# First gates loaded on their own, down weights split earlier, a half's w2 products a step later, beta added in PSUM

## What is computed

```python
# layer 0: per batch, expert weights fside (8 of them) and a shared gate sg
g = einsum('bsd,edf->ebsf', h, Wg);  u = einsum('bsd,edf->ebsf', h, Wu)
expert_outs = einsum('ebsf,efd->ebsd', silu(g) * u, Wd)
x = x + (1 - sg) * einsum('be,ebsd->bsd', gating_probs, expert_outs) \
      + sg * ((silu(h @ Sg) * (h @ Su)) @ Sd)
# layer 1: per batch, by language id
a = relu(x @ W1[lang] + b1[lang]) @ W2[lang] + b2[lang]
z = x + a
x = x + (z - mean(z)) * rsqrt(var(z) + 1e-5) * gamma[lang] + beta[lang]
```

## Time and profile before

| | us |
|---|---|
| median of 3 runs | 300.93 (300.68 to 301.18) |
| the profiled execution | 301.38 |
| its span, first to last instruction | 299.6 |
| PE busy | 291.7 |
| DVE busy | 265.6 |
| ACT busy | 228.6 |
| POOL busy | 18.1 |

### The profile page before, as it was taken

The page is one execution under the profiler, slowest core; times in us unless marked ns, Lnnn a source line. Parts: engine busy times, 40 slices in busy tenths (PEclk is TensorE's granted clock), DMA queues, the critical chain, the costliest instruction groups (busy, mean ns, idle before and its releaser), DMA issues.

```text
span 299.6 us, 5010 instructions
## 1 busy us (share of the span) xinstructions
PE 291.7 (97%) x1518; PEld 145.1 (48%) x1518; DVE 265.6 (89%) x587; ACT 228.6 (76%) x511; POOL 18.1 (6%) x31
## 2 busy tenths in 40 slices
PE   8899999999999999999999999999999999999993
PEld 2344444444444444444444444444444444588782
DVE  4999999998989898988978999989998898977795
ACT  6788888787878787877787788877878775676770
POOL 2200010300000000000001010001100011000001
PEclk9999999999999999999999999999999999999998
DMA  7963031441000000000011001010001100000001
GB/s 204 394 288 109 0 112 24 104 119 47 2 2 0 0 2 0 0 2 1 1 22 20 15 0 38 11 25 16 4 0 40 26 17 9 3 35 3 0 2 35
DMA packets 16620, 12.99 MB, mean 43 GB/s; under 512 B 10818, under 2 KB 14674, under 8 KB 16594
## 3 DMA queue, kind: packets, MB, share of 16 engines
q1 hardware_dynamic: 16162, 12.40, 13.6%
q10 hardware_dynamic: 432, 0.27, 0.3%
HBM read 10.83 MB, written 1.05 MB: 40 GB/s over the span
## 4 chain that ended last, share of the span: by engine, by line
PE 96%; DVE 2%; ACT 1%; issue 0%; POOL 0%; POOLq 0%; DVEq 0%; ACTq 0%
PE gate_ps L374 11%; PE moe_ps L420 10%; PE moe_ps L423 10%; PE moe_ps L421 10%; PE gate_ps L377 10%; PE gate_ps L382 10%; PE up_ps L405 10%; PE up_ps L400 10%; PE up_ps L397 10%; PE moe_ps L455 1%; PE adapt_ps L449 1%; DVE hidden L625 1%; DVE w_lo L611 1%; PE adapt_ps L432 0%; ACT h_hi L529 0%
## 5 line engine op out<-in xcount | busy, mean ns | idle before, releaser
L524 ACT ACTIVATE silu<-gate_ps 128x512 f32<-128x512 f32 (+1 forms) x160 | 88.6, 554 | 58.3 <-PE gate_ps L382 57.4
L625 DVE SCALAR_TENSOR_TENSOR hidden<-silu,up_ps 128x512 f32<-128x512 f32 (+1 forms) x160 | 100.7, 629 | 26.2 <-PE up_ps L405 16.8
L631 DVE TENSOR_TENSOR h_lo<-hidden,h_hi 128x512 f16<-128x512 f32 (+1 forms) x160 | 102.8, 643 | 0.2
L529 ACT ACTIVATE h_hi<-hidden 128x512 f16<-128x512 f32 (+1 forms) x160 | 92.8, 580 | 2.5 <-DVE hidden L625 1.8
L420 PE MATMUL moe_ps<-h_hi,w_hi 128*128 128x512 f16 (+1 forms) x160 | 57.2, 358 | 1.2 <-DVE w_lo L611 1.2
L374 PE MATMUL gate_ps<-x_hi,w_hi 128*128 128x512 f16 (+1 forms) x160 | 57.8, 361 | 0.0
L377 PE MATMUL gate_ps<-x_lo,w_hi 128*128 128x512 f16 (+1 forms) x160 | 57.7, 361 | 0.0
L382 PE MATMUL gate_ps<-x_hi,w_lo 128*128 128x512 f16 (+1 forms) x160 | 57.7, 360 | 0.0
L405 PE MATMUL up_ps<-gx_hi,w_lo 128*128 128x512 f16 (+1 forms) x160 | 57.2, 358 | 0.1
L397 PE MATMUL up_ps<-gx_hi,w_hi 128*128 128x512 f16 (+1 forms) x160 | 57.2, 358 | 0.0
L400 PE MATMUL up_ps<-gx_lo,w_hi 128*128 128x512 f16 (+1 forms) x160 | 57.2, 358 | 0.0
(11 more groups left out here) (74 smaller groups left out, 144.1 us busy)
## 6 DMA issues: line engine op xcount, KB each, us to landing
w_full<-weights SPq DMA_DIRECT2D x8, 768.0 KB, 8.4
affine_sb<-affine SPq DMA_DIRECT2D x16, 128.0 KB, 2.9
x_full<-xT SPq DMA_DIRECT2D x3, 256.0 KB, 8.2
x<-x_blocks SPq DMA_DIRECT2D x48, 16.0 KB, 1.8
out_dram<-result SPq DMA_DIRECT2D x3, 256.0 KB, 2.1
w_full<-weights SPq DMA_DIRECT2D x4, 128.0 KB, 3.4
w2b_sb<-w2b SPq DMA_DIRECT2D x16, 16.5 KB
w_full<-weights SPq DMA_DIRECT2D x1, 256.0 KB, 4.6
```

The costliest lines, as they stand in the source:

```text
L524: nc.scalar.activation(silu_slot(n), gate_ps[n % 2][:, 0:STEPS[n][4]], ACT.Silu, scale=1.0 / W_SCALE).then_inc(silu_ready, 1)
L529: nc.scalar.activation(h_slot(h_hi, n), hidden_slot(n), ACT.Copy).then_inc(h_hi_ready, 1)
L625: nc.vector.scalar_tensor_tensor(out=hidden_slot(n), in0=silu_slot(n), scalar=HIDDEN_RESCALE, in1=up_ps[n % 2][:, 0:STEPS[n][4]], op0=ALU. ...
L631: nc.vector.tensor_tensor(h_slot(h_lo, n), hidden_slot(n), h_slot(h_hi, n), ALU.subtract).then_inc(h_lo_ready, 1)
```

## The change

- The gates are laid out with the shared gate first and then expert by expert. ACT's queue loads the first 32 columns (shared gate and expert 0) first of all, under a semaphore of their own, and then x's second half of tile 0. SP loads x's first half as its second transfer, and the rest of the gates behind weight piece 1. POOL waits for the rest of the gates only before the `coef` of the other experts.
- Weight piece 4 (down weights of expert 0) is split in step 1 on ACT and DVE. Group 1's gated x is made in step 2: on ACT two quarters before `h_hi` of step 1 and two behind it, on DVE all four before `h_lo` of step 1.
- For tile 1 POOL waits for the third `w_lo` only before `x_lo`, not before `x_hi`.
- `back_at` of the last job is 6 instead of 5, and with it `stats_at` and what follows.
- In the tail the transposes of x2 stand behind the w2 products. To each bank a product of a row of ones (row 32 of `adapt_h`) with the beta row is added, and the result reads x2 plus beta from PSUM. DVE's two additions fall away.

```diff
 def back_at(j):
-    return 4 if j < MOVED else 5
+    return 4 if j < MOVED else 6
...
             load_first(0)
-            sp.dma_start(cols(x_full, 1, HALF), xT[0, :, HALF:]).then_inc(x0_loaded[1], 16)
+            sp.dma_start(cols(x_full, 0, HALF), xT[0, :, 0:HALF]).then_inc(x0_loaded[0], 16)
             for i in (1, 2, 3):
                 load_first(i)
+                if i == 1:
+                    sp.dma_start(gates_in[:, 2 * B:], gates[:, 2 * B:]).then_inc(gates_loaded, 16)
...
             for i, q in tail:
-                nc.tensor.transpose(tail_x2_ps[i][:, 0:D], cols(x2T, q, S), ident[:, :]).then_inc(x2_transposed, 1)
-            for i, q in tail:
                 nc.tensor.matmul(tail_y_ps[i][:, 0:D], cols(x2T, q, S), ident[:, :], start=True, stop=False,
                                  is_transpose=True)
...
+            for i, q in tail:
+                nc.tensor.matmul(tail_x2_ps[i][:, 0:D], cols(x2T, q, S), ident[:, :], start=True, stop=False,
+                                 is_transpose=True)
+            for i, q in tail:
+                nc.tensor.matmul(tail_x2_ps[i][:, 0:D], adapt_h[A:A + 1, 0:S],
+                                 cols(affine_sb[A:A + 1], 2 * (last_tile * BATCHES + q) + 1, D, 1),
+                                 start=False, stop=True).then_inc(x2_transposed, 1)
...
-            act.dma_start(cols(x_full, 0, HALF), xT[0, :, 0:HALF]).then_inc(x0_loaded[0], 16)
+            act.dma_start(gates_in[:, 0:2 * B], gates[:, 0:2 * B]).then_inc(first_gates_loaded, 16)
             nc.scalar.preload_act_table(ACT.Silu)
-            act.dma_start(gates_in[:, :], gates).then_inc(gates_loaded, 16)
+            act.dma_start(cols(x_full, 1, HALF), xT[0, :, HALF:]).then_inc(x0_loaded[1], 16)
...
                 silu_of(n)
-                if n == 0:
-                    first_weight_hi(3)
+                if n < 2:
+                    first_weight_hi(3 + n)
                 if n == 2:
-                    first_weight_hi(4)
+                    gated_x_hi(1, 0)
+                    gated_x_hi(1, 1)
                 if n > 0:
                     hidden_hi(n - 1)
-                if n == 1:
-                    gated_x_hi(1, 0)
-                    gated_x_hi(1, 1)
...
-                if n == 0:
-                    first_weight_lo(3)
+                if n < 2:
+                    first_weight_lo(3 + n)
                 if n == 2:
-                    first_weight_lo(4)
+                    for q in range(BATCHES):
+                        gated_x_lo(1, q)
...
-            for i in range(count):
-                tail_x2_beta(i)
...
-                dve.wait_ge(x2_beta_ready, j + i + 1)
-                norm_result(j + i + 1, t, first + i, BEFORE[j] + i + 1)
+                dve.wait_ge(x2_transposed, i + 2)
+                norm_result(j + i + 1, t, first + i, BEFORE[j] + i + 1, tail_x2_ps[i][:, 0:D])
...
-            pool.wait_ge(gates_loaded, 16)
+            pool.wait_ge(first_gates_loaded, 16)
...
                 pool.wait_ge(x_loaded[t - 1], 16)
-                pool.wait_ge(w_lo_ready, X_AFTER[t])
+                if t > 1:
+                    pool.wait_ge(w_lo_ready, X_AFTER[t])
                 nc.gpsimd.tensor_copy(cols(x_hi, t, N), cols(x_full, t, N)).then_inc(x_rest_hi_ready, 1)
                 pool.wait_ge(x_rest_hi_ready, t)
+                if t == 1:
+                    pool.wait_ge(w_lo_ready, X_AFTER[t])
```

More of the change, by code:

```diff
@@ L201, in build @@
         tail_y_ps = [gate_ps[0], up_ps[0]]
+        first_gates_loaded = sem("first_gates_loaded")
         gates_loaded = sem("gates_loaded")
@@ L672, in norm_scaled, with norm_result @@
                                                op0=ALU.subtract, op1=ALU.mult).then_inc(scaled_ready, 1)
-            def norm_result(rstd_done, t, q, done):
+            def norm_result(rstd_done, t, q, done, x2_beta_q):
                 dve.wait_ge(rstd_ready, rstd_done)
@@ L677, in norm_result @@
                 nc.vector.scalar_tensor_tensor(out=cols(result, t * BATCHES + q, D), in0=cols(scaled, q, D),
-                                               scalar=rstd[:, q:q + 1], in1=cols(x2_beta, q, D),
+                                               scalar=rstd[:, q:q + 1], in1=x2_beta_q,
                                                op0=ALU.mult, op1=ALU.add).then_inc(result_ready, 1)
@@ L693, in job_part @@
                         dve.wait_ge(x2_beta_ready, j + 1)
-                        norm_result(j + 1, t, first + i, BEFORE[j] + i + 1)
+                        norm_result(j + 1, t, first + i, BEFORE[j] + i + 1, cols(x2_beta, first + i, D))
                     if since == out_at + i and (j, i) != LATE_OUT:
@@ L747, in _ @@
                                                op1=ALU.add).then_inc(x2T_ready, 1)
-            norm_result(j, late_t, late_q, BEFORE[-1])
+            norm_result(j, late_t, late_q, BEFORE[-1], cols(x2_beta, late_q, D))
             q = first + 1
@@ L777, in _ @@
             pool.wait_ge(ones_ready, 2)
-            pool.wait_ge(gates_loaded, 16)
-            per_expert = gates_in[:, 0:B * (NE - 1)].rearrange("p (b e) -> p e b", b=B)
-            shared_in = gates_in[:, B * (NE - 1):]
+            pool.wait_ge(first_gates_loaded, 16)
+            shared_in = gates_in[:, 0:B]
             nc.gpsimd.tensor_scalar(rest[:, :], shared_in, -X_SCALE, X_SCALE, ALU.mult, ALU.add).then_inc(rest_ready, 1)
             pool.wait_ge(rest_ready, 1)
-            nc.gpsimd.tensor_tensor(coef[:, 0:B], per_expert[:, 0], rest[:, :], ALU.mult).then_inc(first_coef_ready, 1)
+            nc.gpsimd.tensor_tensor(coef[:, 0:B], gates_in[:, B:2 * B], rest[:, :], ALU.mult).then_inc(first_coef_ready, 1)
             nc.gpsimd.tensor_scalar(coef[:, (NE - 1) * B:], shared_in, X_SCALE, None, ALU.mult)
-            nc.gpsimd.tensor_tensor(coef[:, B:(NE - 1) * B].rearrange("p (e b) -> p e b", b=B), per_expert[:, 1:],
+            pool.wait_ge(gates_loaded, 16)
+            nc.gpsimd.tensor_tensor(coef[:, B:(NE - 1) * B].rearrange("p (e b) -> p e b", b=B),
+                                    gates_in[:, 2 * B:].rearrange("p (e b) -> p e b", b=B),
                                     rest[:, :].rearrange("p (o b) -> p o b", o=1).to_broadcast([P, NE - 2, B]),
@@ L845 @@
     wd = wd.reshape(NE, CHUNKS, P, D).transpose(0, 2, 1, 3).reshape(NE, P, F)
-    gates = np.concatenate([a["fside_Bx8_0"].reshape(1, -1), a["condB_sharedgateprob"].reshape(1, B)], axis=1)
+    gates = np.concatenate([a["condB_sharedgateprob"].reshape(1, B), a["fside_Bx8_0"].T.reshape(1, -1)], axis=1)
     arrays = {
```

## The result

The changed kernel takes 299.02 us (median of 6, 298.30 to 299.82), the kernel before 300.81 (median of 6 in the same place): ratio 0.9938, 95% interval 0.992 to 0.9956, 1.79 us less. Run a second time beside other kernels it took 299.41 us, ratio 0.9956 (0.994 to 0.9972). The forecast was 299.54, with 298.7 to 300.3 around it. Three runs far above their like, one of before at 516.83 us beside e1 to e4, one of before at 1091.87 beside e5 to e8 and one of e12 at 311.72, are left out of the ratios.

A forecast was written before the change was run, and what follows sets the result against it. PE is full in the body, so only its idle time at the start, last tile's second half and tail can give: 0.70 + 0.55 + 0.14 = 1.39 us off 300.93, so 299.54 us, range 298.7 to 300.3.

The forecast's parts named there:

- Part 1: Start: splitting down weights ahead of group 1's gated x removes 1.68 us of stall, 0.68 returns, gain 1.00 us.
- the new wait: Start: PE's product L400 of up(4) waits for DVE's fourth gx_lo, giving back 0.68 us.
- Part 2: Start: reordered gates and x loads make later loads land later, taking 0.3 us off the start's 1.00 us gain.
- s: Start: how much later the loads behind the extra gates issue land, 0 to 0.46 us, taken as 0.3.
- the hold: Start: POOL's x_lo of tile 1 holds DVE's 256-wide w_lo, 1.07 us where two take 0.75 us.
- The late first products: Start: first gate products begin 0.1 to 0.3 us later because x's first half is issued later; swallowed right behind hidden(0).
- Part 3: Last tile's second half: w2 products a step later gain 0.55 us (0.3 to 0.75), with 0.17 us waiting at the up product.
- Part 4: Tail: beta in PSUM and later x2 transposes start L492 0.14 us sooner (0 to 0.22); PSUM source costs nothing.
- A: Start: no new wait at L400, or w_lo beats POOL; start gives 1.0 to 1.68 us, time 298.7; chance 0.15.
- B: Start gives only 0.3 us, with later loads, late first product and h_hi(0) slipping; time 300.2 us; chance 0.15.
- C: Start: TensorE's 2.4 GHz level comes later because of the gap before the gate products, eating the gain; 300.9 us; chance 0.05.
- D: Start: ACT stands behind the down weights' load, free up to about 9.2, then one for one; 302.5 us; chance 0.03.

The follow-up runs named there:

- e1: Only the new order of the splits (down weights in step 1, group 1's gated x in step 2) on the kernel before: 299.67 us, ratio 0.9971.
- e4: Only the tail change (x2 transposes behind the w2 products, beta added in PSUM) on the kernel before: 300.47 us, ratio 0.9994.
- e5: New split order, later w2 products and tail change on the kernel before, with loads, gates and POOL's order as before: 299.48 us, ratio 0.9944.
- e8: The changed kernel with a plain fill in place of POOL's x_lo of tile 1: 298.66 us, ratio 0.9922.
- e12: The changed kernel with the down weights issued behind expert 1's 768 KB load: 301.88 us, ratio 1.0037.
- e2: Only the gates and x loads and POOL's order of the changed kernel, on the kernel before: 300.70 us, ratio 0.9993.
- e3: Only the w2 products of the last job one step later, on the kernel before: 300.20 us, ratio 0.9981.
- e7: The kernel before with a plain fill in place of POOL's x_lo of tile 1: 300.25 us, ratio 0.998.
- e6: The changed kernel measured again, unaltered, beside other kernels: 299.41 us, ratio 0.9956 to the kernel before.
- e9: The changed kernel with the rest of the gates loaded behind the down weights and POOL's other coef behind tile 1's x_lo: 299.01 us, ratio 0.9943.

## Why the prediction was right, and where it was off

**Part 1** was right in mechanism and in size within the interval: 1.00 us forecast before the loads' cost, 1.05 measured alone (0.6 to 1.2 by the ratio), 1.12 between the profiles of before and e5. The list of DVE's operations by their own spacing found both the stall that goes and the one that comes back. The size of the new wait was misstated (0.68 us; 0.40 by its own figures, 0.42 measured in e1 and e5), which leaves the gain of 1.00 as it is.

**Part 2** was forecast at minus 0.30 and measured at plus 0.02. The step that failed is s, the later landing of tile 1's x. I took it as fixed, 0.3 us. In the two profiles of the changed kernel POOL's split of that tile starts at 6.95 and at 8.21 us with the same issues, a scatter four times as large as the term; with e2 (7.01) and e8 (7.81) the four start at 7.50 on average. The six with the old loads start between 7.46 and 7.68, 7.57 on average: POOL is no later. The load itself landed 0.2 us later on average (6.9 to 8.2, 7.1 to 7.5 with the old loads), but a term that the forecast put at nothing makes up for it. The forecast read POOL's wait off one profile, where the load ended it; in those of e3, e4, e5 and e7 the load took 4.0 to 4.2 us (landing at 7.1 to 7.3) and POOL stood on for the third `w_lo`, so that the removed wait gives 0.1 to 0.5 us there. So the sum should have carried an unsigned term of up to 0.7 us (the hold, which e7 and e8 price at 0.6 and 0.75), not a loss of 0.3. That is most of the 0.4 us by which the forecast gain of 1.39 fell short of 1.79; the tail (0.20 to 0.25 for 0.14) is the rest. The late first products were smaller than forecast (0.1 to 0.3): 4.48 to 4.74 in the eight profiles with the new loads, 4.58 to 4.66 in the six with the old. What there was of it did not show in the time.

**Part 3** was right: 0.52 us for 0.55, with the short wait at the up product and none at `adapter_back`.

**Part 4** was right in mechanism: one wait less in front of L492, ended by ACT's relu, with the cost of a PSUM source at nothing. The term was mis-sized by 0.06 us, because I put 0.11 us from the relu to the product that it releases, where it is 0.05.

**Rivals.** A came true in part: `w_lo` won the race in the first profile and in e6, but the hold only moved to the next `w_lo` in e6, as the argument against A said. B and C did not come. D's mechanism is real, but its threshold holds only for some executions: it assumed that DVE reaches the down weights at 10.24, as it nearly does in e5 (10.11), but with an early rise and no hold DVE is ready for them at 8.55 (8.82 less the 0.27 us that it waited), and ACT's wait is then on the path. The 8.2 us that D put on the three loads of x is their median and not the time of each: before, that of tile 1, issued just ahead of the down weights, took 4.4 us. The down weights took 4.1 and 4.7 us in the changed kernel's profiles.

**What was luck.** The first profile (298.30 us) is the lowest of the six runs, with an early rise and a hold that missed DVE. The agreement of the medians does not hang on it. But the forecast's two errors of size, the loads and the tail, were both on the cautious side, and the range was wide enough to hold them.

## What to carry over

Write out the queue of the engine that is late by its own spacing, in the new order: it gives what a reordering saves and the wait that comes back behind it (1.00 us forecast, 1.05 measured, 1.12 between two like profiles). Where GpSimd and VectorE both read SBUF, count every two-input VectorE operation that can fall beside a GpSimd one, and carry the hold in the range, because loads that scatter decide which of them it hits. Read what ended a wait from several executions where there are some: here the load ended POOL's in two of six and a `w_lo` in four. And compare two profiles stretch by stretch before explaining a difference of spans: here 3.1 us of span stood for 1.8 us of time.

## What the runs showed of the hardware that I had not expected

- POOL's plain cast of tile 1's x, with one SBUF input, holds a two-input DVE operation as the subtraction does: in e9 a 256-wide `w_lo` beside it takes 0.67 us for 0.42. A fill holds nothing (e7, 0.42 us). It works the other way round too: in e8 the cast that starts 0.13 us after a `w_lo` takes 0.76 us for 0.61.
- The time at which PE's clock rises after the same warm-up differs by some 2 us between executions: 4.2 to 5.4 or 6.7 to 7.3 us, and no profile in between.
- The landing of one and the same load scatters more than a reordering of the queue by one issue (0.45 us) moves it. The down weights took 4.4 to 5.8 us from issue to landing in the six profiles with the old loads, with identical issues, and tile 1's x 3.3 and 4.6 in two of the changed kernel.
